# A decoder layer on one core: the loops over the six middle batches, written out for all five engines

## The chip, the core and the metric

One core of one Trainium2 chip. The metric is the device time of one execution of the whole program, in microseconds (us); smaller is better. The runs shown are separate executions of the same program, and one more execution was taken with the hardware profiler.

## What is computed

A decoder layer over 8 batches of 512 tokens with 256 features, in three parts, each followed by a residual and a layer norm:

```
x = layernorm(x + self_attention(x))            # 16 heads, decayed and level-weighted linear scores, own layer norm inside
x = layernorm(x + cross_attention(x, ctx))      # 16 heads, softmax over 1024 context tokens
x = layernorm(x + experts(x))                   # 32 experts, each picks its top 8 tokens per batch; 256 -> 1024 -> 256, gelu
```

The self attention projects q, k, v and level weights from x, multiplies the causal scores by exp(difference of cumulated decays) and by a weight that depends on the dyadic level of the two positions, and applies the result to v. The cross attention is a plain softmax attention. The experts' part is not touched by the change.

## The kernel before

The kernel is written engine by engine: for each stage a block has one function for each of the five engines (TensorE PE, VectorE DVE, ScalarE ACT, GpSimd POOL, SyncE SP), each with its own instruction stream, and the streams meet only through semaphores that count finished work. The stages are a prologue (decay sums), `self_attention`, `cross_attention`, `experts` and `combine`.

Both attentions go through the 8 batches one after the other, software pipelined, so that in a batch's section the rest of the batch before and the first work of the next one are done as well. The order is written out by hand: `body(sec, b)` emits the instructions of one section, and the helper `sections` (L266) calls it for "pro", "first" (batch 0), "mid" (batches 1 to 6), "last" (batch 7) and "tail". The middle six are one loop of the engine, `eng.Fori(1, B - 1)` (L270), whose body is emitted once and in which `b` is a register: semaphore targets and addresses that depend on b are worked out in registers (small ALU operations, for instance the lines L423 and L427 of PE and L1545 of DVE), and each engine ends the body with an addition and a conditional branch back to its start. There is no barrier between iterations; each engine branches when it gets there. The sections "first" and "last" run the same code as straight instructions with constants.

Self attention, in one batch: 8 steps, one for each pair of heads. In a step PE does the states (L474, tile psA from VP and Kt), the projection of q (L461, psA from xt and wq), the scores (L494), the projection of k (L461 with wk), the far part (L509, L515), a transpose of k (L483) and the near part (L524). Step 0 has the level projection for the next batch as well (L436), steps 2, 3 and 5 have other extras. The q of step 0 of a batch needs the next x, `xt`, which SP loads (L403) as soon as the k projection of step 7 has been done. `states(i, two)` is the first thing PE does in a step, so it stands right behind the loop's branch.

Cross attention, in one batch: 32 steps. In a step PE does the scores (L1324, tile cpsA, 4 matmuls), scores for the row maxima, 12 steps ahead (L1256, cpsV), and the values (L1278, cacc); DVE reduces the maxima (L1553, mx from cpsV), ACT does the exponentials (L1457). Projections and the work on the batch before lie in certain steps. SP stacks the keys and queries with many DMAs (L1143, L1144).

Matmuls on float32 data show up in the profile as two or four instructions for one in the code.

Of the kernel before, what the change touches and what calls it, by code (L numbers as in the profile page):

```python
# [26 lines left out]
B, T, D = 8, 512, 256  # L27
# [235 lines left out]
        return self.index[sec][name]  # L263


def sections(eng, body):  # L266

    body("pro", 0)
    body("first", 0)
    with eng.Fori(1, B - 1) as b:  # L270
        body("mid", b)
    body("last", B - 1)
    body("tail", B)


def flags(sec):

    return sec not in ("pro", "tail"), sec in ("mid", "last", "tail"), sec in ("first", "mid")
# [48 lines left out]
def self_attention(nc, sh, dram):  # L327
    with ExitStack() as ctx:
# [54 lines left out]
        @block.sync  # L383
        def _(sp):
            sp.dma_start(xtv[:], x_of(0)).then_inc(xv_loaded, 16)
            for dst, src in ((wdl, "WdlT"), (wv, "WvT")):
                sp.dma_start(dst[:], dram[src].rearrange("(k p) n -> p k n", p=P)).then_inc(vl_loaded, 16)
            sp.dma_start(lp[:], dram["Lp"].broadcast_to([P, HL])).then_inc(vl_loaded, 16)
            sp.dma_start(xt[:], x_of(0)).then_inc(x_loaded, 16)
            for dst, src in ((wq, "WqT"), (wk, "WkT"), (wo, "WoutT")):  # L390
                sp.dma_start(dst[:], dram[src].rearrange("(k p) n -> p k n", p=P)).then_inc(w_loaded, 16)
            for dst, src in ((lng, "ln_g"), (lnb, "ln_b")):
                sp.dma_start(dst[:], dram[src].broadcast_to([P, D])).then_inc(w_loaded, 16)

            def body(sec, b):
                now, prev, nxt = flags(sec)
                if now and nxt:

                    sp.wait_ge(act_full, SA_ACT.latest(sec, b, (("before", "v", 0), 0)) if prev
                               else SA_ACT.count("pro", 0, ("v", 0)))  # L400
                    sp.dma_start(xtv[:], x_of(b + 1)).then_inc(xv_loaded, 16)
                    sp.wait_ge(act_full, SA_ACT.count(sec, b, ("qk", PAIRS - 1)))
                    sp.dma_start(xt[:], x_of(b + 1)).then_inc(x_loaded, 16)  # L403

            sections(sp, body)
            sp.wait_ge(x_loaded, 16 * B)

        @block.tensor
        def _(pe):
            def body(sec, b):  # L410
# [125 lines left out]
                for i in range(PAIRS if now else 4):  # L536
# [38 lines left out]
                    if i == 3 and prev:  # L575
                        for r in range(2):
# [7 lines left out]
                                                            start=(k == 0), stop=(k == KD - 1))  # L584
                            last.then_inc(dve_full, 1)

            sections(pe, body)
            pe.drain()

        @block.scalar  # L590
        def _(act):
            def body(sec, b):
# [50 lines left out]
                for i in range(PAIRS):  # L643
# [24 lines left out]
                    if i == 7 and prev:  # L668
                        normalise(1)

            sections(act, body)

        @block.gpsimd
        def _(pool):
# [123 lines left out]
                    if i == 7 and prev:  # L798
                        layer_norm_factors(1)

            sections(pool, body)

        @block.vector
        def _(dve):
# [145 lines left out]
                    if i == 7 and nxt:  # L950
                        block_factors()

            sections(dve, body)
            dve.drain()


# [96 lines left out]
def cross_attention(nc, sh, dram):  # L1053
    with ExitStack() as ctx:
# [49 lines left out]
        def parts(eng, ops, n, count):  # L1104


            eng.wait_ge(whole_ready, count)
            if n < 2:
                high, mid, low, r = KP[:, n, 0, :], KP[:, n, 1, :], KP[:, n, 2, :], R[:]
            else:  # L1110
                high, mid, low = QP[:, :, 0, :], QP[:, :, 1, :], QP[:, :, 2, :]
                r = R[:].rearrange("p (h t) -> p h t", h=2)
            zeros = zero[:].broadcast_to([P, KV]) if n < 2 else zero[:].unsqueeze(2).broadcast_to([P, 2, T])
            ops.tensor_tensor(high, r, zeros, ALU.add)  # L1114
            eng.drain()
            ops.tensor_tensor(r, r, high, ALU.subtract)
            eng.drain()
            ops.tensor_tensor(mid, r, zeros, ALU.add)
            eng.drain()
            ops.tensor_tensor(low, r, mid, ALU.subtract)  # L1120
            eng.drain().then_inc(parts_ready, 1)
# [5 lines left out]
        def _(sp):  # L1127
# [63 lines left out]
                        sp.wait_ge(av_done, B * STEPS)  # L1191
                        load_group_weights(sp, sh, dram, 2, 1, EG)

            sections(sp, body)
            sp.wait_ge(p8_saved, 16 * (B + 1))

        @block.tensor
        def _(pe):
# [201 lines left out]
                    if now and (nxt or s + LEAD <= STEPS):  # L1400
                        max_transpose(s + LEAD)

            sections(pe, body)

        @block.scalar
        def _(act):
# [80 lines left out]
                        act.wait_ge(av_done, (bb * QUADS + q + 1) * KT)  # L1487
                        nc.scalar.copy(OT[:], acc[:]).then_inc(acc_evac, 1)

            sections(act, body)  # L1490

        @block.gpsimd
        def _(pool):
            for t in (Vc, NM, P8p, mgp):
                nc.gpsimd.memset(t[:], 0.0)
            pool.drain()
            nc.gpsimd.memset(Vc[:, :, :, HD:HD + 1], 1.0).then_inc(zeroed, 1)
            pool.drain()
            for k in Kst:
                nc.gpsimd.memset(k[ROWS:ROWS + 32], -1.0).then_inc(zeroed, 1)  # L1500
            pool.drain()
            pool.wait_ge(zeroed, 4)

            def add_bo(b):
                nc.gpsimd.tensor_tensor(xb(b), xb(b), bo[:].unsqueeze(1).broadcast_to([P, G, D]), ALU.add
                                        ).then_inc(bo_added, 1)

            def body(sec, b):
                now, prev, nxt = flags(sec)
                if sec == "pro":  # L1510
                    pool.wait_ge(w_loaded, 16 * 5)
                    pool.wait_ge(act_full, CA_ACT.count("pro", 0, "x1T"))
                    add_bo(0)
                if nxt:

                    nc.gpsimd.tensor_tensor(xs[:], xb(b + 1), zero[:].unsqueeze(2).broadcast_to([P, G, D]), ALU.add
                                            ).then_inc(xs_ready, 1)
                    pool.drain()
                    add_bo(b + 1)
                    for q in range(QUADS):  # L1520
                        pool.wait_ge(stacked[q], b * STACKED + STACKED)
                    parts(pool, nc.gpsimd, 2, b * 3 + 4)
                if prev:
                    pool.wait_ge(var, b)
                    nc.gpsimd.tensor_tensor(rstd[:, :, 0], mv[:, :, 1], sh.eps[:, 0:G], ALU.add)  # L1525
                    pool.drain()
                    nc.gpsimd.tensor_tensor(rstd[:, :, 0], rstd[:, :, 0], sh.mhalf[:, 0:G], ALU.pow).then_inc(rstd_ready, 1)
                if nxt:
                    parts(pool, nc.gpsimd, 0, b * 3 + 5)
                    parts(pool, nc.gpsimd, 1, b * 3 + 6)  # L1530

            sections(pool, body)

        @block.vector
        def _(dve):
# [112 lines left out]
                    if now and (nxt or s + LEAD <= STEPS):  # L1648
                        max_rows(s + LEAD)

            sections(dve, body)

# [299 lines left out]
```

## Time and profile before

| | us |
|---|---|
| three runs | 2046.22, 2048.55, 2045.87 |
| median | 2046.22 |
| the profiled execution, its own time | 2049.28 |
| its span, first to last instruction | 2047.5 |
| self attention, all 8 batches (on PE) | about 62 to 676 |
| cross attention, maxima and all 8 batches (on PE) | about 730 to 1822 |
| experts and combination | about 1850 to 2047.5 |

The times in the profile are counted from the first instruction. PE is busy 1773.0 us of the span, DVE 1267.0, ACT 858.7 and POOL 540.2. A line in the form "L474 ... [4.98 <-issue]" says that the engine stood idle for 4.98 us before this instruction and that no semaphore of another engine ended the idle time; "DMA" or another engine's name there is who did.

### The profile page before, as it was taken

How to read it: one execution, taken by the hardware profiler on the slowest of the kernel's cores; microseconds unless marked ns; L12 is line 12 of the kernel's file. 1: busy time of each engine (PE TensorE's matmuls, PEld its weight loads, DVE VectorE, ACT ScalarE, POOL GpSimd, SP SyncE). 2: the span in 40 equal slices, each digit the busy share in tenths (PEclk: the TensorE clock that was granted, in tenths of full speed). 3: DMA queues.
4: the chain of work that ended last, by engine and by line, in shares of the span. 5: the costliest groups of instructions: out<-in, count | busy, mean ns of one | idle time of the engine just before them, and what ended most of it. 6: DMA issues, size and time to landing. Idle time of an engine off the chain costs nothing. (4 is left out here: it accounts for less than half of the span.)

```text
span 2047.5 us, 50339 instructions
## 1 busy us (share of the span) xinstructions
PE 1773.0 (87%) x19756; PEld 848.5 (41%) x19756; DVE 1267.0 (62%) x2435; ACT 858.7 (42%) x1031; POOL 540.2 (26%) x650
## 2 busy tenths in 40 slices
PE   4799999989899569999999999999999999976566
PEld 2466656556556313333343333333433433322224
DVE  4666566566565386877867867778678678821005
ACT  0334234243243114554545645545456446551113
POOL 0535445445342513214023032140130310000002
PEclk7899999999899659999999999989999999997675
DMA  5200000000000121110111101201111013145982
GB/s 177 81 24 21 6 24 19 8 24 7 20 14 4 45 81 34 55 60 25 48 44 48 51 17 48 67 15 56 45 48 39 29 48 127 67 184 218 422 356 96
DMA packets 64422, 143.34 MB, mean 70 GB/s; under 512 B 11376, under 2 KB 34448, under 8 KB 56048
## 3 DMA queue, kind: packets, MB, share of 16 engines
q1 hardware_dynamic: 59504, 136.29, 18.4%
q10 hardware_dynamic: 4736, 4.46, 0.6%
q8 instruction: 134, 2.20, 0.4%
q14 instruction: 48, 0.39, 0.1%
HBM read 97.59 MB, written 4.98 MB: 50 GB/s over the span
## 5 line engine op out<-in xcount | busy, mean ns | idle before, releaser
L1553 DVE TENSOR_REDUCE mx<-cpsV 128x1 f32<-128x512 f32 x1024 | 651.4, 684 | 224.9 <-PE cpsV L1256 211.6
L1457 ACT ACTIVATE w<-cpsA 128x1024 f32<-128x1024 f32 x512 | 496.3, 1021 | 372.8 <-PE cpsA L1324 372.7
L1256 PE MATMUL cpsV<-w 96*128 96x512 bf16 x1024 | 339.0, 402 | 64.4 <-DVE mx L1553 50.3
L1278 PE MATMUL cacc<-w 128*32 128x512 f32 x2048 | 281.5, 615 | 0.4 <-ACT w L1457 0.4
L1324 PE MATMUL cpsA<-w 99*128 99x512 bf16 x1024 | 276.0, 392 | 0.3
L1256 PEld LDWEIGHTS cpsV<-w 96*128 96x128 bf16 x1024 | 84.8, 99 | 379.6 <-DVE mx L1553 220.8
L1114 POOL TENSOR_TENSOR w<-w,zero 128x1024 bf16<-128x1024 f32 x21 | 39.7, 1892 | 643.5 <-ACTq L1430 643.5
L649 ACT COPY QK<-psA 128x1024 f32<-128x1024 f32 x64 | 64.8, 1012 | 252.9 <-PE psA L461 252.9
L1324 PEld LDWEIGHTS cpsA<-w 99*128 99x128 bf16 x1024 | 98.0, 99 | 127.3 <-ACT w L1457 11.9
L461 PE MATMUL psA<-xt,wq 128*128 128x512 f32 x256 | 137.4, 662 | 7.4 <-ACT QK L649 3.0
L739 POOL TENSOR_TENSOR VP<-V,VPF 128x128 f32<-128x128 f32 (+2 forms) x256 | 125.1, 519 | 60.3 <-PE psA L474 57.2
L461 PE MATMUL psA<-xt,wk 128*128 128x512 f32 x256 | 128.1, 623 | 2.7 <-DVE WT L907 2.6
L916 DVE TENSOR_TENSOR tmp<-psV,CF 128x512 f32<-128x512 f32 x64 | 44.2, 691 | 137.9 <-PE psV L524 137.6
L1778 DVE TENSOR_TENSOR z<-psHT,b1T 128x256 f32<-128x256 f32 x8 | 3.4, 425 | 128.4 <-PE psHT L1736 128.4
L1278 PEld LDWEIGHTS cacc<-w 128*32 128x32 f32 x2048 | 42.3, 109 | 97.2 <-issue 81.0
L474 PE MATMUL psA<-VP,Kt 128*64 128x64 f32 (+2 forms) x1280 | 53.1, 229 | 30.2 <-issue 27.0
L923 DVE TENSOR_REDUCE Y<-tmp 128x128 f32<-128x512 f32 x64 | 67.5, 1055 | 4.7
L1525 POOL TENSOR_TENSOR crstd<-cmv,eps 128x4 f32<-128x4 f32 x8 | 1.6, 201 | 250.4 <-DVE cmv L224 250.4
L461 PEld LDWEIGHTS psA<-xt,wq 128*128 128x128 f32 x256 | 46.3, 201 | 46.3 <-issue 38.4
L494 PEld LDWEIGHTS psV<-QK 64*32 64x32 f32 x4096 | 41.7, 108 | 52.3 <-issue 52.1
L1429 ACT COPY w<-cpsA 128x1024 f32<-128x1024 f32 x24 | 24.3, 1012 | 91.6 <-PE cpsA L1226 49.8
L474 PEld LDWEIGHTS psA<-VP,Kt 128*64 128x64 f32 x1280 | 45.1, 144 | 38.9 <-issue 34.4
(214 smaller groups left out, 2417.7 us busy)
## 6 DMA issues: line engine op xcount, KB each, us to landing
w<-in_w SPq DMA_DIRECT2D x64, 1024.0 KB, 16.9
w<-w SPq DMA_DIRECT2D x192, 128.0 KB, 2.3
w<-w SPq DMA_DIRECT2D x192, 64.0 KB, 2.0
w<-in_ctxT SPq DMA_DIRECT2D x8, 1024.0 KB, 5.1
pro_xt<-in_xT SPq DMA_DIRECT2D x8, 512.0 KB, 7.1
x_tok<-in_x SPq DMA_DIRECT2D x8, 512.0 KB, 9.1
xtv<-in_xT SPq DMA_DIRECT2D x8, 512.0 KB, 4.8
xt<-in_xT SPq DMA_DIRECT2D x8, 512.0 KB, 3.7
```

The lines of the kernel that those rows point to most:

```text
L461: last = nc.tensor.matmul(out[:, n * T:(n + 1) * T], w[:, k, i * P:(i + 1) * P], xt[:, k, :], start=(k == 0), stop=(k == KD - 1))
L474: last = nc.tensor.matmul(out[r, HD * slot:HD * (slot + count)], Kt[:, g * P + S * hh:g * P + S * hh + S], VP[:, p % 2, g, column:column + ...
L494: last = nc.tensor.matmul(out[j * BLK:(j + 1) * BLK, at:at + BLK], QK[r, p % 4, T + t0:T + t0 + BLK], QK[r, p % 4, t0:t0 + BLK], start=Tru ...
L649: nc.scalar.copy(QK[:, i % 4, :], full(("qk", i))).then_inc(act_evac, 1)
L739: last = nc.gpsimd.tensor_tensor(VP[:, p % 2, g, 0:n, :].rearrange("q n (h c) -> q n h c", c=HD), vv.unsqueeze(1).broadcast_to([P, n, 2, HD]),
L916: nc.vector.tensor_tensor(tmp[:].rearrange("p g s (h c) -> p (g s) h c", c=HD), src.rearrange("p (h x) -> p h x", h=2)[:, :, 0:4 * HD * G] ...
L923: nc.vector.tensor_reduce(yp, tmp[:].rearrange("p g s c -> p g c s"), AX_X, ALU.add)
L1256: nc.tensor.matmul(out, Qst[q // 2][0:ROWS, hh, g * P:(g + 1) * P], Kst[q // 2][0:ROWS, hh, half * BANK:(half + 1) * BANK], start=True, st ...
L1278: last = nc.tensor.matmul(acc[BLK * jj:BLK * (jj + 1), :], Vc[:, c, 4 * q + jj, :], Pr[:, (2 * s + jj // 2) % 4, (jj % 2) * T:(jj % 2 + 1) ...
L1324: last = nc.tensor.matmul(out[:, n * T:(n + 1) * T], Kst[q // 2][0:ROWS + 3, hh, c * P:(c + 1) * P], Qst[q // 2][0:ROWS + 3, hh, :], start ...
L1457: nc.scalar.activation(Pr[:, (2 * s + pp) % 4, :], src, ACT.Exp, scale=CA_SCALE).then_inc(act_evac, 1)
L1553: nc.vector.tensor_reduce(mx[:, q % 2, row, k % 2:k % 2 + 1], full(m[k]), AX_X, ALU.max).then_inc(dve_evac, 1)
```

## The change

`sections` gets a switch. With it, the six middle sections are emitted one after the other with b as a plain number, and all ten callers (five engines in the self attention, five in the cross attention) set it. Nothing else is changed: no operation, tile, buffer or order of work.

```diff
-def sections(eng, body):
+def sections(eng, body, unrolled=False):
+
 
     body("pro", 0)
     body("first", 0)
-    with eng.Fori(1, B - 1) as b:
-        body("mid", b)
+    if unrolled:
+        for b in range(1, B - 1):
+            body("mid", b)
+    else:
+        with eng.Fori(1, B - 1) as b:
+            body("mid", b)
     body("last", B - 1)
     body("tail", B)
...
-            sections(sp, body)
+            sections(sp, body, unrolled=True)
...
-            sections(pe, body)
+            sections(pe, body, unrolled=True)
...
-            sections(act, body)
+            sections(act, body, unrolled=True)
...
-            sections(pool, body)
+            sections(pool, body, unrolled=True)
...
-            sections(dve, body)
+            sections(dve, body, unrolled=True)
```

What stands in PE's stream between step 7 of one middle batch and step 0 of the next in the self attention. Before, step 7 ends with the near part (L524) and then comes the loop's end; after the jump PE is at the loop's first rows, of which the second piece shows the start:

```order
L461 MATMUL psA<-xt,wk 128x512 x2
L509 MATMUL psV<-Mst,QK 64x64 x12
L509 MATMUL psV<-Mst,QK 64x48 x4
L515 MATMUL psV<-Mst,QK 64x16 x4
L483 MATMUL psA<-ident,QK 128x128 x4
L524 MATMUL psV<-V,WT 32x16 x32
L270 REGISTER_ALU
L270 COMPARE_AND_BRANCH
```

```order
L270 ISA
L470 ISA
L474 MATMUL psA<-VP,Kt 64x64 x2
L474 MATMUL psA<-VP,Kt 64x16 x2
L474 MATMUL psA<-VP,Kt 64x64 x4
L474 MATMUL psA<-VP,Kt 64x48 x2
L423 ISA
L427 REGISTER_ALU
L547 ISA
L461 MATMUL psA<-xt,wq 128x512 x2
```

And after the change, at the same join (batch 2 to batch 3, lines five higher):

```order
L488 MATMUL psA<-ident,QK 128x128 x4
L529 MATMUL psV<-V,WT 32x16 x32
L479 MATMUL psA<-VP,Kt 64x64 x2
L479 MATMUL psA<-VP,Kt 64x16 x2
L479 MATMUL psA<-VP,Kt 64x64 x4
L479 MATMUL psA<-VP,Kt 64x48 x2
L466 MATMUL psA<-xt,wq 128x512 x2
L499 MATMUL psV<-QK 32x32 x32
L466 MATMUL psA<-xt,wk 128x512 x2
```

The matmuls and their order are the same; the branch, its addition and the register rows (51 REGISTER_ALU rows in PE's body of the self attention, 224 in that of the cross attention) are gone, and the semaphore waits carry constants.

What stands in DVE's stream at the end of a middle batch in the cross attention, where it reduces maxima; before:

```order
L1553 TENSOR_REDUCE mx<-cpsV 128x1
L1545 REGISTER_ALU
L1553 TENSOR_REDUCE mx<-cpsV 128x1
L1545 REGISTER_ALU
L1553 TENSOR_REDUCE mx<-cpsV 128x1
L270 REGISTER_ALU
L270 COMPARE_AND_BRANCH
```

and after the change, in a row from one of these stretches on:

```order
L1579 COPY nmT<-cpsV 48x128
L1558 TENSOR_REDUCE mx<-cpsV 128x1 x2
L1615 TENSOR_TENSOR o<-cpsV,x_tok 128x256 x4
L221 BN_STATS cstats<-o 128x6 x4
L224 BN_AGGR cmv<-cstats 128x2 x4
L1558 TENSOR_REDUCE mx<-cpsV 128x1 x8
L1622 TENSOR_SCALAR o<-o,cmv,crstd 128x256 x4
L1558 TENSOR_REDUCE mx<-cpsV 128x1 x8
```

A row before each reduction went, and the loop's end with it; the reductions follow each other directly.

The program grows: PE's stream has 1156 such rows before and 2015 after, DVE's 735 and 1082, ACT's 442 and 545, POOL's 255 and 509, SP's 276 and 534 (a row with x stands for that many instructions).

## Rows read from the trace of the kernel before

**Rows 1.** The page: busy time of the engines.
```profile
PE 1773.0 (87%) x19756; PEld 848.5 (41%) x19756; DVE 1267.0 (62%) x2435; ACT 858.7 (42%) x1031; POOL 540.2 (26%) x650
```

**Rows 2.** Waits of PE: what waited, releaser, us in total, times, longest.
```profile
PE psA L474 <- issue: 27.0, 5, 6.2
```

**Rows 3.** Line L270, 200 to 600 us (self attention): durations ns min/median/max, first and last start.
```profile
L270 PEldq COMPARE_BRANCH  x6: 82/4963/6067, 202.4 to 590.0; - x6
L270 POOLq COMPARE_BRANCH  x6: 40/45/50, 202.5 to 590.0; - x6
...
L270 DVEq COMPARE_BRANCH  x6: 50/56/67, 208.0 to 596.1; - x6
```

**Rows 4.** Timeline of PE around jumps back in the self attention.
```profile
196.02 1.98 PE L461 MATMUL psA<-xt,wq 128*128 128x512 f32 x4
...
207.53 1.31 PE L474 MATMUL psA<-VP,Kt 128*64 128x64 f32 x20 [4.98 <-issue]
208.77 3.78 PE L461 MATMUL psA<-xt,wq 128*128 128x512 f32 x4
...
220.42 1.98 PE L461 MATMUL psA<-xt,wq 128*128 128x512 f32 x4
...
530.72 1.98 PE L461 MATMUL psA<-xt,wq 128*128 128x512 f32 x4
```

**Rows 5.** Timeline of PE where batches meet without a jump (0 to 1).
```profile
124.91 1.98 PE L461 MATMUL psA<-xt,wq 128*128 128x512 f32 x4
...
133.53 1.99 PE L461 MATMUL psA<-xt,wq 128*128 128x512 f32 x4 [1.21 <-DMA xt<-in_xT]
...
140.06 2.44 PE L436 MATMUL psA<-wdl,xtv 128*128 128x160 f32 x16
...
143.28 1.98 PE L461 MATMUL psA<-xt,wq 128*128 128x512 f32 x4
150.62 1.98 PE L461 MATMUL psA<-xt,wq 128*128 128x512 f32 x4
```

**Rows 6.** The same, batch 6 to 7, with DVE's first product of batch 7.
```profile
592.11 3.65 PE L461 MATMUL psA<-xt,wq 128*128 128x512 f32 x4 [1.11 <-DMA xt<-in_xT]
...
596.49 0.42 DVE L907 TENSOR_TENSOR WT<-psV,LF 128x256 f32<-128x256 f32 x1 [0.54 <-PE psV L494]
...
601.04 1.98 PE L461 MATMUL psA<-xt,wq 128*128 128x512 f32 x4
608.31 1.98 PE L461 MATMUL psA<-xt,wq 128*128 128x512 f32 x4
```

**Rows 7.** Stretches: us, PE busy (count), PEld, DVE, ACT, POOL, granted clock, DMA share, GB/s.
```profile
131.50:142.50 11.00, 9.76 (x218) 6.67 (x220) 7.57 (x16) 1.96 (x3) 1.55 (x4) 1.00 0.25 84
206.50:213.30 6.80, 5.77 (x88) 3.09 (x88) 1.33 (x3) 0.36 (x1) 1.50 (x4) 0.50 0.01 2
592.20:595.60 3.40, 3.40 (x4) 0.98 (x4) 3.17 (x9) 0.45 (x2) 3.19 (x10) 0.50 0.02 5
```

**Rows 8.** Line L270, 1020 to 1600 us (cross attention), the jumps back.
```profile
L270 PEldq COMPARE_BRANCH  x5: 207/208/244, 1026.5 to 1579.1; - x5
```

**Rows 9.** Waits of DVE, 1025 to 1720 us.
```profile
DVE mx L1553 <- issue: 10.2, 5, 2.2
```

**Rows 10.** Timeline of PE: scores of steps 0 and 2, batches 1, 2 and 6.
```profile
889.40 1.03 PE L1324 MATMUL cpsA<-w 99*128 99x512 bf16 x4
...
900.67 1.03 PE L1324 MATMUL cpsA<-w 99*128 99x512 bf16 x4
...
1027.25 1.03 PE L1324 MATMUL cpsA<-w 99*128 99x512 bf16 x4
...
1591.32 1.03 PE L1324 MATMUL cpsA<-w 99*128 99x512 bf16 x4
```

**Rows 11.** DMA queues (packets, MB, share): 200 to 600 us, then 750 to 1030 us.
```profile
q8 instruction: 77, 1.26, 1.3%
...
q8 instruction: 11, 0.18, 0.3%
```

More of the change, by code:

```diff
@@ L1192, in body @@
                         load_group_weights(sp, sh, dram, 2, 1, EG)
-            sections(sp, body)
+            sections(sp, body, unrolled=True)
             sp.wait_ge(p8_saved, 16 * (B + 1))
@@ L1401, in body @@
                         max_transpose(s + LEAD)
-            sections(pe, body)
+            sections(pe, body, unrolled=True)
         @block.scalar
@@ L1488, in body @@
                         nc.scalar.copy(OT[:], acc[:]).then_inc(acc_evac, 1)
-            sections(act, body)
+            sections(act, body, unrolled=True)
         @block.gpsimd
@@ L1530, in body @@
                     parts(pool, nc.gpsimd, 1, b * 3 + 6)
-            sections(pool, body)
+            sections(pool, body, unrolled=True)
         @block.vector
@@ L1649, in body @@
                         max_rows(s + LEAD)
-            sections(dve, body)
+            sections(dve, body, unrolled=True)
 def experts(nc, sh, dram):
```

## The prediction

> **What bounds the kernel now.** I first read the busy times of the page [rows 1]: PE is busy for 1773.0 us of a span of 2047.5, DVE for 1267.0, and the others far less. In both attentions the kernel is worth what PE's stream is worth, so the question is what the loops cost PE.
>
> The view of PE's waits [rows 2] gives the first answer: before the states matmul (L474) PE stands idle five times for 27.0 us, the longest 6.2, and the releaser is "issue": no semaphore of another engine ended it. L474 is the first work behind the loop's start, and a loop of six iterations jumps back five times. The rows of the loop's own line say what it is [rows 3]: PE's conditional branch takes 82 ns at the least (the sixth, which falls through) and up to 6067 ns, while DVE's takes 50 to 67. The reader is to see the ends of the range, not the median alone: the time is in PE's taken branches, and in PE's alone.
>
> Then I asked how much of 5 us reaches the batch. I measure from the q projection of step 1 of one batch to that of the next: 220.42 less 143.28 is 77.14 us for the first, and from 143.28 to 530.72, five of these periods, 387.44, or 77.49 each [rows 4, 5]. In each lies one jump back. The same period without a jump can be put together from rows of the same trace: steps 1 to 6 of batch 1 take 196.02 - 143.28 = 52.74 (to the start of step 7), and step 7 and step 0 where batch 0 runs straight into batch 1 take 143.28 - 124.91 = 18.37 [rows 4, 5]. Together 71.11. With the jump, step 7 and step 0 took 220.42 - 196.02 = 24.40.
>
> **Where the 6.0 us of the first jump come from.** The idle time is 4.98 [rows 4]. Against it stands a wait that the jump hides: with no jump PE waits 1.21 us for the DMA that brings xt [rows 5], 1.11 at the other straight join [rows 6]; behind a jump the data is there. The rest is the clock: right after the stall the granted clock is 0.50 (1.2 GHz) for 6.8 us [rows 7], and the q projection takes 3.78 where it takes 1.99 at 2.4 GHz [rows 4, 5], and L474 takes 1.31 [rows 4]. So 4.98 - 1.21 = 3.77, and 6.03 - 3.77 = 2.26 for the clock. A reader who counts only the 27.0 us of stalls would be near the right sum by accident: 6 us of it come back as the xt wait, and 11 are added by the clock.
>
> **The change, part by part.**
>
> 1. *Five jumps back of PE in the self attention go.* 387.44 - 5 x 71.11 = 31.9 us off. All of it is on the path, since the measure is from PE work to PE work. What is late next is xt: 1.2 us at each join, already in the 18.37.
>
> 2. *Five jumps of DVE in the cross attention go.* Behind each DVE is idle for some 2 us that no semaphore ends (10.2 us over five times) [rows 9]. PE's own branch there costs 207 to 244 ns [rows 8] and its queue covers that. How much of DVE's 2 us reaches PE? From the scores of step 0 to those of step 2: 900.67 - 889.40 = 11.27 where batch 1 is entered without a jump [rows 10]. Five whole periods, 1591.32 - 900.67 = 690.65, stand against 5 x (1027.25 - 900.67 + 11.27) = 689.25: 1.4 us off. The maxima are made 12 steps ahead, which covers the rest.
>
> 3. *The register operations go.* Steps 1 to 2 of the self attention in a middle batch take 150.62 - 143.28 = 7.34, in the last batch, which has constants, 608.31 - 601.04 = 7.27 [rows 5, 6]: 0.07. Bounds: nothing, if the 0.07 is the work for the next batch that the last one lacks; 48 steps x 0.07 = 3.4 us at the most. I take 1.0, since other steps have other ends. In the cross attention I take nothing: the waits there are covered by queued matmuls.
>
> 4. *The clock at the new joins.* A wait of 1.1 to 1.2 us stays at each, in the stretch of small matmuls between two projections. At the join of batches 0 and 1 the granted clock stays at 1.00 (2.4 GHz); at that of 6 and 7 it is 0.50 for 3.4 us, and the q projection takes 3.65 instead of 1.99, 1.66 more [rows 5 to 7]. The two known joins differ, and nothing in the rows says which the five new ones follow. Bounds: 0 and 5 x 1.66 = 8.3. I take the middle, two or three of them: +4.2.
>
> 5. *Instructions have to be brought in.* The change's own cost: the five repeated bodies of each loop are now different instructions. For PE in the self attention this costs nothing new, since it fetches already: 77 blocks in 400 us, some 15 a batch [rows 11], one every 5 us, with the steps at 7.34. For PE in the cross attention it is new: straight sections fetch 11 blocks in 280 us [rows 11], the loop none, so some 5 to 6 a batch and 28 more in all, one in 25 us. I cost them at nothing; what hides them is that they are fetched ahead of use, at a fifth of the rate that the self attention sustains. If that cover fails, a late block costs what a jump costs, about 5 us.
>
> 6. *Launch, experts, combination, SP's and POOL's streams:* the same operations, DMAs and order; their branches take some 0.05 us each [rows 3] beside PE's work. Nothing.
>
> Sum: -31.9 - 1.4 - 1.0 + 4.2 = -30.1 us. Against the profiled execution, 2049.28 - 30.1 = 2019.2. That one lies 3.1 above the median of the runs, 2046.22, so I put the predicted median at **2016.1 us**.
>
> **A rule weighed against the rows.** In the cross attention PE's taken branch costs 0.2 us and no block is fetched in its loop [rows 8]. The Trainium skill (Runtime: NRT & Kernel Launch, Instruction fetch mechanics) says that a taken branch whose target is outside a window of two pages forces a fetch before execution goes on, and that there is no cache beyond it. By that rule PE's long cross-attention body would stall at each jump too. It doesn't here; the page's rule fits the self attention alone.
>
> **The rivals.**
>
> *A new wait at the middle joins (4%).* Only middle joins have both the layer norm of the batch before at step 7 and the level projection at step 0. Before, the stall gave DVE 5 us to finish its block factors. At the join of 6 and 7 DVE still waited 0.54 us for PE's scores, with that layer norm in step 7 [rows 6], so it keeps up by a small margin. If it were late by 2 us and PE waited at each join, 10 us of the gain would go: 2026.
>
> *The jumps of the cross attention stall PE as well, hidden behind other waits (2%).* If each cost PE what it costs in the self attention, five times 6.4 or 32 us more would go: 1984. Against it: the branch rows [rows 8] and 1.4 us in five periods [rows 10]. It is what the rule of the Trainium skill's page above gives.
>
> *The streams are not fed in time (3%), slower than before.* The cross attention also moves the stacked keys and queries by DMA, and now all five engines fetch there. If two blocks a batch came late in six batches, each for 5.4 us (27.0 / 5 [rows 2]), that is 65 us: 2016 + 65 = 2081. It decides from six late blocks on, where 30 us are eaten up. Against it: the straight sections of the cross attention fetch beside the same DMAs [rows 11] and go from step 0 to step 2 in 11.27, faster than the loop.
>
> *Nothing changes (1%).* If the stall belonged to the place in memory and not to the jump, it would come again at a block's start: 2046. Against it: the sixth branch of the same code falls through in 82 ns [rows 3], and the two straight joins have no such idle time.
>
> **How the numbers follow.** The forecast, 90%: the jumps' cost goes, its size is uncertain by points 2 to 4. Best case: -31.9 - 1.4 - 3.4 and no drop of the clock, with that of the join of 6 and 7 gone too (-1.7), is -38.4: 2008. Worst case: 0 for points 2 and 3 and a clock cost of 2.26 at each of five joins, as behind a stall, is -31.9 + 11.3 = -20.6: 2026, which takes in the first rival. So the range is 2008 to 2026. A change of about 0.2%, 4 us, is what a measurement can tell here. Faster by more than that: 0.95 (forecast, first and second rival, less a remainder). Within: 0.02. Slower: 0.03.
>
> **What would show it right or wrong.** In the profile of the changed kernel: no idle time "issue" of 5 us before the states matmul, but a wait for the DMA of xt of about 1.2 us before seven q projections; periods of 71.1 us between the q projections of steps 1, or 72.8 where the clock drops; half clock in the self attention for 3.4 us at some joins instead of 6.8 or more at all; periods of the cross attention of about 137.9; more blocks in the fetch queue, some 28 for PE. Wrong would be: an "issue" wait of microseconds at other places of PE, DVE or ACT; DVE as releaser of PE's scores or near part at the joins; or periods above 74 us in the self attention.

## The result, and the profile after

| | before | after |
|---|---|---|
| median of the runs on one chip, us | 2047.37 (2045.87 to 2048.55, 4 runs) | 2033.68 (2030.6 to 2036.72, 4 runs) |
| the profiled execution, its own time | 2049.28 | 2033.99 |
| its span | 2047.5 | 2032.2 |

The ratio is 0.9933, with a 95% interval of 0.9916 to 0.9951: 13.7 us less, between 10 and 17. The kernel is faster, as forecast, but by less than half of the forecast 30.1 us, and 2033.7 lies outside the range of 2008 to 2026.

Lines of the changed kernel are five higher: L474 is L479, L461 is L466, L1324 is L1329, L1256 is L1261, L1553 is L1558.

The page of after, against [rows 1] and the queue of instruction fetches, which had 134 packets before:

```profile
PE 1765.8 (87%) x19756; PEld 844.0 (42%) x19756; DVE 1289.7 (63%) x2435; ACT 858.9 (42%) x1031; POOL 544.4 (27%) x650
...
q8 instruction: 151, 2.47, 0.5%
```

PE is busy 7.2 us less (less time at half clock). DVE is busy 22.7 us more with the same 2435 operations. Of these, 9.8 us are in three tiny operations of the cross attention (45.4 us before, 55.2 after), which is the first sign of what went wrong. Another 11.3 are in products on `lam` in the self attention; they are as long in the first experiment below, which is faster.

The waits of PE in after (us in total, times, longest), against [rows 2]:

```profile
PE cpsV L1261 <- DVE mx L1558: 57.9, 48, 3.9
...
PE psA L466 <- DMA xt<-in_xT: 10.3, 6, 2.7
```

The five waits "issue" of 27.0 us before the states matmul are gone. In their place stands the wait for xt, 10.3 us over six of the seven joins, the longest 2.7 where the two joins known before had 1.21 and 1.11. And there is a wait of up to 3.9 us on DVE's maxima in the cross attention.

**The joins of the self attention.** Timeline of PE in after around the first four joins, against [rows 4, 5]; in each pair that stands together the second row is the q projection of step 0:

```profile
126.03 1.98 PE L466 MATMUL psA<-xt,wq 128*128 128x512 f32 x4
...
136.03 3.52 PE L466 MATMUL psA<-xt,wq 128*128 128x512 f32 x4 [2.65 <-DMA xt<-in_xT]
...
147.40 1.95 PE L466 MATMUL psA<-xt,wq 128*128 128x512 f32 x4 [0.21 <-ACT DL L609]
...
206.53 0.79 PE L479 MATMUL psA<-VP,Kt 128*64 128x64 f32 x20
...
210.00 2.92 PE L466 MATMUL psA<-xt,wq 128*128 128x512 f32 x4 [2.67 <-DMA xt<-in_xT]
...
282.27 3.50 PE L466 MATMUL psA<-xt,wq 128*128 128x512 f32 x4 [1.16 <-DMA xt<-in_xT]
...
354.73 1.95 PE L466 MATMUL psA<-xt,wq 128*128 128x512 f32 x4 [1.11 <-DMA xt<-in_xT]
```

The reader is to see that L479 now takes 0.79 us with no idle time before it, where behind the jump it took 1.31 behind 4.98. The q projection has two forms: 1.95 at full clock, 2.92 to 3.52 where part of it ran at half clock. The windows of after say the same at three of the new joins (us, PE busy, PEld, DVE, ACT, POOL, granted clock, DMA share, GB/s), against [rows 7]:

```profile
211.20:214.60 3.40, 3.40 (x69) 1.52 (x68) 1.62 (x3) 0.00 (x0) 0.92 (x2) 0.55 0.03 7
...
355.00:361.00 6.00, 6.00 (x176) 3.29 (x176) 3.88 (x10) 1.75 (x4) 3.21 (x10) 1.00 0.06 21
...
426.30:429.70 3.40, 3.40 (x37) 0.94 (x37) 3.04 (x7) 0.00 (x0) 2.79 (x8) 0.56 0.03 9
```

Of the five new joins three drop to about 0.55 (near 1.2 GHz) for 3.4 us, two do not. Step 7 with step 0, which was 24.40, 23.63, 25.26, 24.73 and 25.49 us at the five jumps (123.51 together), is 21.19, 19.90, 18.24, 20.19 and 18.55 (98.07): 25.4 us less. The join that has never had a jump, batch 0 to 1, went from 18.37 to 147.40 - 126.03 = 21.37, 3.0 us more. Steps 1 to 6 of the six middle batches together went from 316.8 to 315.6 us, 0.19 us a batch.

**The cross attention.** Timeline of PE, first scores of batches 1 and 7 in after, against 889.40 in [rows 10] and the row of before that stands behind it:

```profile
866.51 1.03 PE L1329 MATMUL cpsA<-w 99*128 99x512 bf16 x4
...
1705.72 1.03 PE L1329 MATMUL cpsA<-w 99*128 99x512 bf16 x4
```

```profile
1717.73 1.03 PE L1324 MATMUL cpsA<-w 99*128 99x512 bf16 x4
```

Six periods took 1717.73 - 889.40 = 828.33 us, 138.06 each, and take 839.21, 139.87 each: **10.9 us more**, where 1.4 less was forecast. Step by step the largest difference in each period is step 12: it takes 7.42 us where it took 5.69, 10.4 us in six periods. The other steps moved both ways, from +3.8 us (step 5) to -1.7 (step 14) in six periods, and come to 0.5 together.

Where the 15.3 us of the span lie:

| us | forecast | measured |
|---|---|---|
| five joins with a jump, clock included | -27.7 | -25.4 |
| joins 0 to 1 and 6 to 7 | 0 | +3.0, -1.6 |
| steps 1 to 6, register operations | -1.0 | -1.1 |
| start and tail of the self attention | 0 | +1.1, +1.7 |
| cross attention, batch 0 | 0 | -0.6 |
| cross attention, six periods | -1.4 | +10.9 |
| last batch, experts, combination | 0 | -3.2 |
| sum | -30.1 | -15.2 |

Of the 14.8 us that are missing, 12.3 are in the row of the six periods. Its mechanism can be read in one step 12 of before and the same one of after. First before, timeline of PE, ACT, POOL and DVE (start us, duration us; the bracket is the idle time ahead of it and its releaser):

```profile
1090.70 1.07 PE L1278 MATMUL cacc<-w 128*32 128x512 f32 x8
...
1090.88 1.01 ACT L1429 COPY w<-cpsA 128x1024 f32<-128x1024 f32 x1 [4.39 <-PE cpsA L1226]
...
1092.01 1.89 POOL L1114 TENSOR_TENSOR w<-w,zero 128x1024 bf16<-128x1024 f32 x1 [9.74 <-ACTq L1430]
1092.13 1.29 DVE L1553 TENSOR_REDUCE mx<-cpsV 128x1 f32<-128x512 f32 x2 [2.56 <-PE cpsV L1256]
...
1094.02 0.17 DVE L1562 TENSOR_TENSOR nr<-nm,NM 128x16 f32<-128x16 f32 x1
1094.04 2.14 POOL L1116 TENSOR_TENSOR w<-w 128x1024 f32<-128x1024 f32 x1
1094.11 2.10 DVE L1563 TENSOR_TENSOR NM<-nm,NM 128x16 bf16<-128x16 f32 x1
...
1096.29 0.18 DVE L1565 TENSOR_TENSOR NM<-nr,NM 128x16 bf16<-128x16 f32 x1
...
1096.32 1.90 POOL L1118 TENSOR_TENSOR w<-w,zero 128x1024 bf16<-128x1024 f32 x1
...
1097.15 0.44 PE L1256 MATMUL cpsV<-w 96*128 96x512 bf16 x1 [2.23 <-DVE mx L1553]
```

Then after:

```profile
1070.60 1.07 PE L1283 MATMUL cacc<-w 128*32 128x512 f32 x8
1070.71 1.01 ACT L1434 COPY w<-cpsA 128x1024 f32<-128x1024 f32 x1 [4.39 <-PE cpsA L1231]
...
1071.83 1.89 POOL L1119 TENSOR_TENSOR w<-w,zero 128x1024 bf16<-128x1024 f32 x1 [9.72 <-ACTq L1435]
1072.03 1.29 DVE L1558 TENSOR_REDUCE mx<-cpsV 128x1 f32<-128x512 f32 x2 [2.56 <-PE cpsV L1261]
...
1073.87 2.12 POOL L1121 TENSOR_TENSOR w<-w 128x1024 f32<-128x1024 f32 x1
1073.91 2.11 DVE L1567 TENSOR_TENSOR nr<-nm,NM 128x16 f32<-128x16 f32 x1
...
1076.13 1.89 POOL L1123 TENSOR_TENSOR w<-w,zero 128x1024 bf16<-128x1024 f32 x1
...
1076.18 1.88 DVE L1570 TENSOR_TENSOR NM<-nr,NM 128x16 bf16<-128x16 f32 x1
...
1078.71 0.61 PE L1261 MATMUL cpsV<-w 96*128 96x512 bf16 x1 [3.90 <-DVE mx L1558]
```

DVE has three tiny operations on 128x16 here, of two inputs each, that turn the maxima into three bf16 parts; POOL has four operations on 128x1024, back to back, that cut the keys in parts. Alone a tiny one takes 0.17 us. One that starts while POOL is inside its operation ends with POOL's: L1563 from 1094.11 to 1096.21, POOL's from 1094.04 to 1096.18. Before, the first of the three starts 0.02 us *ahead* of POOL's second operation and slips through, and so does the third (1096.29), 0.03 ahead of POOL's third (1096.32): one of the three is held. After, the first starts 0.04 us *behind* POOL's second and the third (1076.18) 0.05 behind POOL's third (1076.13), and these two are held, for 2.11 and 1.88 us. It is so in all six middle batches of both kernels. PE, which waits for maxima behind them, stands 3.90 us instead of 2.23.

What moved is ACT. Its copy of k starts 0.18 us behind PE's L1278 before and 0.11 us behind L1283 after. The register operation that worked out its semaphore's target is gone, and in batch 0 of the kernel before, which has a constant there, the copy is 0.11 behind too. POOL, which waits for that copy, gains the same, and now runs 0.20 us ahead of DVE's first maximum instead of 0.12. Faster by 0.07 us, later by 1.7. The longer wait was there to be seen in the kernel before: batch 0 is straight code, and in its step 12 (timeline of PE, before) PE stood as long as it does now.

```profile
826.40 0.61 PE L1256 MATMUL cpsV<-w 96*128 96x512 bf16 x1 [3.89 <-DVE mx L1553]
```

The Trainium skill (SBUF — State Buffer, SBUF: two separate sides) says that DVE and GpSimd share a pair of ports by an exclusive lock which is held for the whole instruction. The trace agrees with its number: an operation of 0.17 us takes 2.10 beside one of 2.14.

### The profile page after: what moved, and what is told of

The parts are those of the page before. It is cut to its first block and busy times, and to the rows that moved or that the text cites. A ratio compares the mean times of both kernels' runs of the same rounds, so it can differ in the third digit from the quotient of the medians.

```text
span 2032.2 us, 46769 instructions
## 1 busy us (share of the span) xinstructions
PE 1765.8 (87%) x19756; PEld 844.0 (42%) x19756; DVE 1289.7 (63%) x2435; ACT 858.9 (42%) x1031; POOL 544.4 (27%) x650
## 3 DMA queue, kind: packets, MB, share of 16 engines
q1 hardware_dynamic: 59504, 136.29, 18.5%
HBM read 97.59 MB, written 4.98 MB: 50 GB/s over the span
## 5 line engine op out<-in xcount | busy, mean ns | idle before, releaser
L1558 DVE TENSOR_REDUCE mx<-cpsV 128x1 f32<-128x512 f32 x1024 | 651.8, 684 | 226.5 <-PE cpsV L1261 223.9
L1261 PE MATMUL cpsV<-w 96*128 96x512 bf16 x1024 | 340.9, 405 | 72.3 <-DVE mx L1558 57.9
L1283 PE MATMUL cacc<-w 128*32 128x512 f32 x2048 | 282.4, 617 | 0.4 <-ACT w L1462 0.4
L1329 PE MATMUL cpsA<-w 99*128 99x512 bf16 x1024 | 277.3, 393 | 0.3
L1261 PEld LDWEIGHTS cpsV<-w 96*128 96x128 bf16 x1024 | 84.8, 100 | 386.1 <-DVE mx L1558 223.3
L1329 PEld LDWEIGHTS cpsA<-w 99*128 99x128 bf16 x1024 | 99.1, 100 | 129.2 <-issue 12.4
L466 PE MATMUL psA<-xt,wq 128*128 128x512 f32 x256 | 132.6, 642 | 18.3 <-DMA xt<-in_xT 10.3
L744 POOL TENSOR_TENSOR VP<-V,VPF 128x128 f32<-128x128 f32 (+2 forms) x256 | 130.5, 542 | 41.2 <-PE psA L479 38.1
L466 PE MATMUL psA<-xt,wk 128*128 128x512 f32 x256 | 128.2, 623 | 2.6 <-DVE WT L912 2.6
L1283 PEld LDWEIGHTS cacc<-w 128*32 128x32 f32 x2048 | 42.3, 109 | 97.7 <-issue 83.0
L466 PEld LDWEIGHTS psA<-xt,wq 128*128 128x128 f32 x256 | 44.8, 195 | 55.5 <-issue 49.9
L1231 PE MATMUL cpsA<-w,w 128*128 128x512 f32 x128 | 58.6, 602 | 2.6 <-ACT w L1462 2.6
L1248 PE MATMUL cpsA<-w,w 128*128 128x128 f32 x512 | 60.0, 275 | 0.8 <-ACT w L1434 0.7
```

Of the source, the lines that this page charges most:

```text
L466: last = nc.tensor.matmul(out[:, n * T:(n + 1) * T], w[:, k, i * P:(i + 1) * P], xt[:, k, :], start=(k == 0), stop=(k == KD - 1))
L744: last = nc.gpsimd.tensor_tensor(VP[:, p % 2, g, 0:n, :].rearrange("q n (h c) -> q n h c", c=HD), vv.unsqueeze(1).broadcast_to([P, n, 2, HD]),
L1231: last = nc.tensor.matmul(out[:, n * BANK:(n + 1) * BANK], wk[:, k, hk * P:(hk + 1) * P], cT[:, k, n * BANK:(n + 1) * BANK], start=(k == 0 ...
L1248: last = nc.tensor.matmul(out[:, c * P:(c + 1) * P], cT[:, k, c * P:(c + 1) * P], wv[:, k, hv * P:(hv + 1) * P], start=(k == 0), stop=(k = ...
L1261: nc.tensor.matmul(out, Qst[q // 2][0:ROWS, hh, g * P:(g + 1) * P], Kst[q // 2][0:ROWS, hh, half * BANK:(half + 1) * BANK], start=True, st ...
L1283: last = nc.tensor.matmul(acc[BLK * jj:BLK * (jj + 1), :], Vc[:, c, 4 * q + jj, :], Pr[:, (2 * s + jj // 2) % 4, (jj % 2) * T:(jj % 2 + 1) ...
```

## The experiments

Theory A: the self attention gains what its joins show and the cross attention loses by the order of POOL's and DVE's operations, which ACT's missing register operation turned. The rivals are named where they are tested. No kernel leaves out any part of the computation. Unless another is shown, an edit consists of which of the ten callers of `sections` have `unrolled=True`. Ratios are against the kernel before on the same chip, with the 95% interval. The chips differ: the median of the kernel before is 2044.0 us beside the first four experiments, 2043.5 beside the next four and 2046.7 beside the last three, and after was measured beside 2047.4. So a difference in us to after can be off by some 5 us, and the profiled executions are compared stretch by stretch.

**One attention alone.** Only the self attention written out, all five engines:

```diff
 # the five callers in cross_attention
-            sections(pe, body, unrolled=True)
+            sections(pe, body)
```

> Only the self attention is written out; all five engines keep their loop in the cross attention. Theory A (the two attentions went opposite ways: the self attention saves 23.6 us by PE's start of the cross attention, and writing out the cross attention costs 1.8 us in each of six batches because one more small DVE operation is held up by a POOL operation): the cross attention's period is 138.1 us again, PE's gap before the maxima scores at step 12 is 2.2 us and not 3.9, and the time is 11 us below the changed kernel, 25 below before: about 2022. Rival B (the self attention saves little in most executions, and the cross attention's longer period belongs to where the self attention ends, not to its own code): 2034 and periods of 139.9.

Measured: 2024.87 us (2016.63 to 2028.33), ratio 0.9899 (0.9881 to 0.9917). Step 7 with step 0 took 18.1 to 18.6 at all seven joins in the profiled execution. At six of them the q projection took 1.95 us; at the last, behind a wait of 2.13 us for xt, it took 3.06, with a granted clock of 0.50 from 562 to 564 us. The periods of the cross attention are 137.4 to 139.5, and step 12 takes 5.69 in each of the six. So half of the change is worth more than the whole, by 7 us in the ratios, whose intervals just touch. The spread of 12 us over its runs fits joins at which the clock drops in one execution and not in another; only one of them was profiled, so that is read from one execution.

Only the cross attention written out:

```diff
 # the five callers in self_attention
-            sections(pe, body, unrolled=True)
+            sections(pe, body)
```

> Only the cross attention is written out. Theory A: slower than before by 9 to 11 us, 2056 to 2058, with periods of 139.9 us and the 3.9 us gap in each of six batches; PE's five stalls of 5 us stay in the self attention. Rival B (the code of the cross attention does not matter): 2047, periods of 138.1.

Measured: 2056.35 us (2054.13 to 2059.64), ratio 1.0057 (1.0043 to 1.0071): slower than before. Periods 139.7 to 140.1. The DMA queues of this kernel between 1020 and 1700 us, against the loop, which fetched nothing there:

```profile
q8 instruction: 26, 0.43, 0.3%
```

26 more blocks for PE, and no idle time "issue" of PE above 0.1 us in the middle batches. The rival that fetching makes the loss would want waits of 5 us. The next pair of experiments rules it out as well: with PE's stream written out and ACT's not, PE fetches the same blocks and the loss is gone.

**One engine alone.** All written out but ACT in the cross attention, and then the reverse: the self attention and of the cross attention ACT alone.

```diff
 # e3: in cross_attention
-            sections(act, body, unrolled=True)
+            sections(act, body)
 # e4: in cross_attention, the other four (pe, dve, pool, sp)
-            sections(pe, body, unrolled=True)
+            sections(pe, body)
```

> All written out but ACT's loop in the cross attention. Theory A in its sharp form: what moved is ACT, which no longer computes a semaphore target in a register before its copy of the k projection, so POOL starts 0.07 us earlier against DVE's chain of five small operations, and two of them instead of one wait for a POOL operation of 2.1 us. With ACT's loop back the copy is late again: gap at step 12 of 2.2 us, periods of 138.1, about 2022. Rival C (DVE's own register operations, or PE's, set the alignment): the 3.9 us gap and periods of 139.9 stay, 2034.

> The self attention written out, and in the cross attention ACT alone. Theory A in its sharp form: ACT alone brings the 3.9 us gap at step 12, periods of 139.9 and 2034. Rival C: periods of 138.1 and about 2022, as with all five loops kept.

Measured: 2026.4 us (2021.81 to 2030.95), ratio 0.991 (0.9892 to 0.9927), and 2033.44 (2028.06 to 2036.67), ratio 0.9943 (0.9927 to 0.9959). Their medians lie 7.0 us apart. The six periods, which the clock at the joins does not touch, take 826.6 us in the first and 139.5 to 139.95 each, 839.1, in the second: 12.6 apart. The first kernel loses 5.2 us of that again behind the last scores (see point 6 below); from the first scores of batch 1 to the end it is 1158.2 against 1165.6, 7.4 us. Timeline of a step 12 with ACT in its loop:

```profile
1204.89 1.06 PE L1283 MATMUL cacc<-w 128*32 128x512 f32 x8
1205.07 1.01 ACT L1434 COPY w<-cpsA 128x1024 f32<-128x1024 f32 x1 [4.39 <-PE cpsA L1231]
...
1208.21 0.17 DVE L1567 TENSOR_TENSOR nr<-nm,NM 128x16 f32<-128x16 f32 x1
1208.23 2.14 POOL L1121 TENSOR_TENSOR w<-w 128x1024 f32<-128x1024 f32 x1
```

And with ACT alone written out:

```profile
1209.42 1.07 PE L1283 MATMUL cacc<-w 128*32 128x512 f32 x8
1209.53 1.01 ACT L1434 COPY w<-cpsA 128x1024 f32<-128x1024 f32 x1 [4.39 <-PE cpsA L1231]
...
1212.69 2.12 POOL L1121 TENSOR_TENSOR w<-w 128x1024 f32<-128x1024 f32 x1
1212.74 2.10 DVE L1567 TENSOR_TENSOR nr<-nm,NM 128x16 f32<-128x16 f32 x1
```

ACT's copy 0.18 us behind PE's start and DVE 0.02 ahead of POOL, or 0.11 behind and DVE 0.05 late. ACT's stream alone sets it, with the other four all written out or all in loops, and in each of the six batches. This settles the cause of the longer periods.

**PE in the self attention alone**, the other nine callers with their loops:

```diff
 # all callers but sections(pe, ...) in self_attention
-            sections(dve, body, unrolled=True)
+            sections(dve, body)
```

> PE's stream in the self attention alone is written out; every other loop stays. Theory A (the gain is PE's taken branch and the clock behind it, nothing of the other four): all of the self attention's gain comes, steps 7 and 0 together take 18.4 to 20.5 us instead of 24 to 25.5, no idle time 'issue' of 5 us before the states, and the time is that of e1: 2018 to 2028. Rival D (the other engines' loops matter as much, SP's above all, whose register operations put the load of xtv 0.9 us behind that of xt, against 0.4 when written out): not below 2030.

Measured: 2021.21 us (2018.22 to 2023.67, 4 runs), ratio 0.989 (0.9866 to 0.9915). Step 7 with step 0: 21.05, 19.32, 18.29, 18.21, 17.88, 17.91, 16.89. The gain is in PE's stream: the other four bring nothing that these runs can tell. The rival D, that the long waits for xt come from SP, which without register operations issues the second load (xtv) sooner behind xt, falls: with SP in its loop the waits are 2.30 and 2.24 at the first two joins and 2.31 at the last all the same. The closer loads are real, as SP's timeline at the first join shows, before and then after, but they are not the cause:

```profile
129.52 0.38 SPq L403 DMA_DIRECT2D xt<-in_xT  x1
130.29 0.40 SPq L401 DMA_DIRECT2D xtv<-in_xT  x1
```

```profile
130.65 0.38 SPq L408 DMA_DIRECT2D xt<-in_xT  x1
131.07 0.48 SPq L406 DMA_DIRECT2D xtv<-in_xT  x1
```

Why xt lands 1 us later at some joins than at others stays open.

**Taking the lock apart.** If one tiny operation is held as long as POOL's operation lasts, shorter ones on POOL must give the time back. Each of POOL's four is cut into four on a quarter of the columns:

```diff
-            ops.tensor_tensor(high, r, zeros, ALU.add)
-            eng.drain()
...
+            pieces = 4 if ops is nc.gpsimd else 1
+            width = (KV if n < 2 else T) // pieces
+
+            def each(out, a, c, op):
+                for j in range(pieces):
+                    at = slice(j * width, (j + 1) * width)
+                    ops.tensor_tensor(out[..., at], a[..., at], c[..., at], op)
+                return eng.drain()
+
+            each(high, r, zeros, ALU.add)
```

> The changed kernel, with each of POOL's 2.1 us operations on the parts of keys and queries cut in four pieces along the columns. Theory A (a small two-input DVE operation waits until POOL's running operation has ended, and PE and then its clock pay for it): DVE's held-up operations fall from 2.1 to about 0.6 us, PE's gaps of 2.3 and 3.9 us in each batch of the cross attention to under 1 us, the drops of the clock behind them go, and the period falls from 139.9 to between 131 and 135: 2033 less 35 to 60, or about 1980 to 2000. Rival E (POOL pays more for twelve more operations per part, the parts come late, and PE waits for the stacked keys): periods of 140 or more, 2035 or slower.

Measured: 2004.67 us (2003.31 to 2007.11), ratio 0.9817 (0.9797 to 0.9836). That is 29 us less than after by the medians and 24 by the ratios, and in the profiled executions the six periods take 811.1 us instead of 839.2. It is 5 above what was expected: the periods are 136.5 for the most part. The mechanism holds, and a second place of it came up. Timeline of DVE, POOL and PE in this kernel (lines ten higher than before):

```profile
1196.97 2.55 POOL L1125 TENSOR_TENSOR w<-w 128x256 f32<-128x256 f32 x4
1197.03 0.65 DVE L1573 TENSOR_TENSOR NM<-nm,NM 128x16 bf16<-128x16 f32 x1
...
1205.09 2.20 DVE L1644 TENSOR_TENSOR P<-L 32x512 f32<-32x512 f32 x1
...
1206.90 2.59 POOL L1515 TENSOR_TENSOR x_tok<-x_tok,bo 128x1024 f32<-128x1024 f32 x1 [0.16 <-issue]
1207.37 2.41 DVE L1646 TENSOR_SCALAR P<-P,rsum 32x512 f32<-32x512 f32 x1
...
1210.43 0.61 PE L1266 MATMUL cpsV<-w 96*128 96x512 bf16 x1 [3.82 <-DVE mx L1563]
```

The held operation takes 0.65 us instead of 2.10, beside pieces of 2.55 / 4 = 0.64. But behind step 12 DVE now meets two other long operations of POOL (one of them L1515, of 2.59), and takes 2.20 and 2.41 us for operations that take 0.66 and 0.47 in after: PE waits 3.82 us there.

**The wait for xt taken away.** xt gets two buffers, and SP loads the next x five steps earlier:

```diff
-                sp.wait_ge(act_full, SA_ACT.count(sec, b, ("qk", PAIRS - 1)))
-                sp.dma_start(xt[:], x_of(b + 1))
+                sp.wait_ge(act_full, SA_ACT.count(sec, b, ("qk", 2)))
+                sp.dma_start(xt[:, (b + 1) % 2], x_of(b + 1))
```

> The changed kernel with two buffers for xt, the next one loaded from step 2 of the batch before. Theory A (what is left at the joins is the wait for xt of 1.1 to 2.7 us, and the half clock that sometimes follows): no wait for the DMA of xt, steps 7 and 0 together 17.2 us at all joins, the self attention 10 to 18 us shorter, 2016 to 2023. Rival F (DVE's block factors become the bound at the joins, or the clock falls in the stretch of small matmuls also without a wait): steps 7 and 0 stay at 18.4 or above, 2028 to 2034.

Measured: 2015.22 us (2013.78 to 2017.1), ratio 0.9868 (0.9848 to 0.9887), 0.8 us below the expected stretch. The wait for xt is gone from PE's list, step 7 with step 0 takes 17.1 us at each of six joins and 14.53 at the last, and the clock stays up. Window of this kernel at a join:

```profile
269.00:272.00 3.00, 2.98 (x103) 2.25 (x95) 1.59 (x3) 2.12 (x5) 2.58 (x7) 1.00 0.02 5
```

That is 18.5 us less than after by the medians and 13 by the ratios. In the profiled executions the seven joins take 117.1 us together instead of 135.4, where the waits put down to xt were 10.3 us: the rest is what the clock and the work around the join took. Without the wait the q projection takes 1.98 us at every join; with it, the clock can drop (four of seven joins in after, the last in the first experiment) or not. The spread of the runs is not explained by it: it is 3.3 us here and 12 in the first experiment, but 8.5 in the fastest version below, which doesn't wait for xt either.

**Together, and further.** Both edits; then POOL's two other long operations in quarters as well:

```diff
-                nc.gpsimd.tensor_tensor(xb(b), xb(b), bo[:].unsqueeze(1).broadcast_to([P, G, D]), ALU.add
-                                        ).then_inc(bo_added, 1)
+                for g in range(G):
+                    last = nc.gpsimd.tensor_tensor(xb(b)[:, g, :], xb(b)[:, g, :], bo[:], ALU.add)
+                last.then_inc(bo_added, 1)
```

> Both edits together. Theory A: the gains add, since they lie in different stages: 1965 to 1985. If E or F holds for one of them, only the other's gain shows.

> Both edits, and POOL's two other long operations in a batch of the cross attention (the copy of x and the added bias, 1.9 and 2.6 us) cut in four as well. Theory A: in e6 and e8 these two held up DVE's subtraction and scaling at the top-8 step by 2.2 and 2.4 us, with 3.8 us of idle PE behind them in most batches; cut in four they hold it for some 0.6 us each, the 3.8 us gap goes, and the period falls from 136.5 to 130 to 132 in all batches: 1984 less 15 to 30, 1955 to 1970. Rival G (the top-8 step is late for another reason, its own chain): 136.5 stays, 1984.

Measured: 1984.38 us (1984.14 to 1988.89), ratio 0.972 (0.970 to 0.974): the two gains add. The six periods take 811.1 us, as with the cut alone, and the joins 17.1 and 14.53, as with two buffers alone; by the medians, 2033.7 - 29.0 - 18.5 = 1986.2. Then 1966.15 us (1961.61 to 1970.1), ratio 0.961 (0.9594 to 0.9626), **the fastest version, 3.9% under the kernel before**. Its periods are 133.0 for the most part, 1 to 3 above what was expected. Its page and its longest wait on DVE's maxima:

```profile
PE 1732.3 (88%) x19756; PEld 831.1 (42%) x19756; DVE 1263.2 (64%) x2435; ACT 858.6 (44%) x1031; POOL 592.8 (30%) x947
```

```profile
PE cpsV L1266 <- DVE mx L1565: 34.1, 48, 1.5
```

DVE does the same 2435 operations in 26.5 us less than in after. POOL is busy 48 us more, for 297 instructions more, and the end comes earlier all the same.

**Is the writing out needed for that?** First the cut of POOL's parts in the kernel before, with all loops; then the kernel of both edits with the loops of the cross attention put back.

> The kernel before, all loops kept, with POOL's parts operations cut in four. Theory A: what the cut is worth does not hang on the loops; one held-up pair is already gone in the loop form, so the period falls from 138.1 to about 136.5 and the first batch gains its 4 us: 2044 less 12 to 25, 2019 to 2032. Rival H (the cut helps only the written-out form): 2044.

> As e8 (cut parts, two xt buffers), but the cross attention keeps its loops on all engines. Theory A: with the parts cut, 0.07 us more or less on ACT no longer decides over 2 us, so this is within 6 us of e8: 1978 to 1990. Rival I (the written-out cross attention costs time for another reason, fetching for instance): 10 us or more below e8, 1974 or less.

Measured: 2023.13 us (2021.93 to 2023.49, 4 runs), ratio 0.9886 (0.9871 to 0.9901): the cut alone brings more than the change under study. And 1989.35 (1983.8 to 1991.72), ratio 0.9717 (0.9702 to 0.9732), against 1984.38 with everything written out; the runs of the two overlap and their ratios are the same. With short operations on POOL, the form of the cross attention's loops is worth nothing that these runs can tell; in the profiled executions the six periods take 814.6 us with the loops and 811.1 without.

## Why the prediction was wrong

The points are those of the prediction.

*1. The five jumps of PE.* Right in mechanism and nearly in size. All of the "issue" waits went, and where the clock stayed up the new joins took 18.2 and 18.6, as the known one with its clock up (18.37). The first experiment had 18.1 to 18.6 at all of them.

*2 and 3. The cross attention: the step that failed.* "In the cross attention I take nothing: the waits there are covered by queued matmuls", and the five periods of point 2 at -1.4. Measured +10.9 over six periods, of which some 3 come back behind the last scores (point 6). The jumps of DVE did go, and batch 1 is no slower in steps 0 to 2; but removing register operations was taken for something that can only gain or do nothing. It moves engines against each other by 0.07 us, and in step 12 two engines that share a resource stood 0.02 us from the other order. The bounds should have had a loss in them, and its price stood in the trace: batch 0, the same step in straight code, had a step 12 of 7.41 where the loop had 5.69. The prediction compared straight code and loop over steps 0 to 2 only and called the rest equal. Six times 1.73 is 10.4: with it the forecast would have been 2026.5, still 7 under the median.

In the self attention point 3 was right: 0.19 a batch, 1.1 together, against 1.0.

*4. The clock.* Right in kind, short in size. Two or three drops were forecast at the five new joins, three came. But the new joins were costed by the two known ones and their wait for xt of 1.1 to 1.2; it is up to 2.67. The five joins stand 6.2 us over 5 x 18.37 instead of 4.2, and the first join, costed at nothing because it has no jump, lost 3.0 by the same wait and a drop of its own.

*5. Fetching instructions.* Right. "28 in all" for PE in the cross attention, 26 measured; no stall. (That the loop there fetches nothing isn't in [rows 8], which are the branches; the trace of before has no packet in PE's fetch queue from 1020 to 1600 us.) The page's count rose by 17 only, since in the self attention the loop had fetched more than the straight code does (the first experiment has 125 packets, 9 fewer than before).

*6. The rest at nothing.* The last batch and the experts came out 3.2 us shorter in the profiled pair. The steps of batch 7 are as long as before; the product `cpsV<-cwo,oT` behind them takes 5.41 us at a granted clock of 0.68 before and 3.72 at 1.00 after, and a further 1.5 us are gained behind it. This goes with the form of ACT's stream: it takes 3.72 in the four kernels that have ACT written out in the cross attention and POOL's operations whole, with 225 us from the last scores to the end, and 5.2 to 6.5 in all others, with 227 to 230 us. So what ACT's written-out stream costs is less than its six periods say: 7.6 us, from 1158.1 to 1165.7 between the first scores of batch 1 and the end. Why the clock is higher there stays open.

*The rivals.* None of them was what happened. The sign of the fetching rival (slower in the cross attention) was right, its cause was not. The rule that the jumps of the cross attention stall PE too would have made those periods shorter by 6.4 us; they grew.

*The signs to look for.* "Periods of the cross attention of about 137.9" was the right thing to watch: 139.87 is what showed the error at first sight. The periods of the self attention, forecast at 71.1, or 72.8 with a drop, came out at 72.2 on average (52.61 + 98.07 / 5).

Of the 14.8 us missing, the clock and the longer waits at the seven joins account for 3.7 (2.3 + 3.0 - 1.6), the cross attention's periods for 12.3; start and tail of the self attention took 2.8, and batch 0 and the end gave 3.8 back; the 0.2 left over are the registers' 0.1 and rounding.

## What to carry to other kernels

Look at the shortest rows, not only the longest: an operation that takes 0.17 us in one batch and 2.10 in another beside one of a neighbour's that lasts 2.1 points at a shared resource, and here shortening the neighbour's operation gave the time back. When a change makes code of one kind into another (loop into straight code), compare the whole period wherever both kinds already run, step by step, before calling the rest equal. And a removed instruction off the critical path is not free of cost by that: ask whose order it decides.

## What the runs showed of the hardware

- A DVE operation with two inputs on 128x16 takes 0.17 us alone and ends with POOL's when it starts inside one on 128x1024: 2.10 beside 2.14. Cut in quarters, POOL's operations hold it 0.65. A CAST on 128x16, with one input, was held once in the kernel before as well: it took 1.65 us instead of 0.17, from 784.22 to 785.87, inside a POOL operation that ended at 785.85. A TENSOR_SCALAR of DVE on 32x512, with one tensor as input, took 2.41 us beside a POOL operation of 2.59, and 0.47 without.
- Taking one register operation from ACT's stream moves its next operation from 0.18 to 0.11 us behind the matmul. The written-out form of ACT's stream alone made the cross attention 1.8 us a batch slower, by an order that 0.02 to 0.05 us decided, and 7.4 us slower from batch 1 to the end.
- PE's taken branch left it idle for 4.8 to 6.2 us in the self attention's loop and cost 0.2 in the cross attention's. Straight code that needs 26 more blocks for PE ran with no stall, one block in some 26 us.
- A wait of 1.1 to 2.7 us in a stretch of small matmuls was followed at some joins by about 3.4 us at or near half clock (0.55 and 0.56 in two windows of after), at others by none, and which ones changed between kernels. In the profiled executions without the wait the q projection took its 1.98 us at every join.
